# Folding row pairs in place one pass ahead, instead of inside the forward line transform

## What is computed

```python
xf = jnp.fft.rfft2(x, axes=(1, 2), norm='ortho')          # H and W; W keeps 65 modes
xf = xf.reshape(b, h, wf, NUM_BLOCKS, BLOCK)              # 8 blocks of 96 channels
o1r = relu(xr @ w1[0] - xi @ w1[1] + b1[0])               # per block, 96x96
o1i = relu(xi @ w1[0] + xr @ w1[1] + b1[1])
o2r = o1r @ w2[0] - o1i @ w2[1] + b2[0]
o2i = o1i @ w2[0] + o1r @ w2[1] + b2[1]
o2r, o2i = softshrink(o2r, 0.01), softshrink(o2i, 0.01)
out = jnp.fft.irfft2(xc, s=(H, W), axes=(1, 2), norm='ortho') + x
```

## Time and profile before

| what | value |
|---|---|
| median of three runs | 5846.9 us (5845.65 to 5852.03) |
| the profiled execution's own time | 5840.84 us |
| its span, first to last instruction | 5838.6 us |
| busy share of TensorE matmuls, VectorE, ScalarE, GpSimd | 93%, 62%, 35%, 36% |
| mean granted TensorE clock | 0.976 of full speed |

### The profile page before, as it was taken

The page is one execution under the profiler, slowest core; times in us unless marked ns, Lnnn a source line. Parts: engine busy times, 40 slices in busy tenths (PEclk is TensorE's granted clock), DMA queues, the critical chain, the costliest instruction groups (busy, mean ns, idle before and its releaser), DMA issues.

```text
span 5838.6 us, 114567 instructions
## 1 busy us (share of the span) xinstructions
PE 5407.1 (93%) x44352; PEld 4374.4 (75%) x44352; DVE 3593.4 (62%) x5379; ACT 2044.7 (35%) x3504; POOL 2079.6 (36%) x1572
## 2 busy tenths in 40 slices
PE   7999999999999999999999999999999999999998
PEld 6777777778777777777777777777777777777777
DVE  4666566665666656666566665566655666556665
ACT  2333333333333333333333333333333333333333
POOL 3442234422344323443234432344322343223432
PEclk9999999999999999999999999999999999999999
DMA  3331133311333213332133321233312333113311
GB/s 95 88 92 44 48 88 88 92 45 48 88 88 92 55 37 88 88 92 68 30 82 88 92 75 31 75 88 92 87 28 65 88 92 88 40 53 88 92 45 44
DMA packets 1065694, 421.18 MB, mean 72 GB/s; under 512 B 1062816, under 2 KB 1062944, under 8 KB 1065120
## 3 DMA queue, kind: packets, MB, share of 16 engines
q1 hardware_dynamic: 1060384, 411.62, 26.4%
q10 hardware_dynamic: 4736, 1.60, 0.1%
HBM read 210.26 MB, written 201.33 MB: 70 GB/s over the span
## 4 chain that ended last, share of the span: by engine, by line
PE 48%; issue 31%; DVE 12%; POOL 8%; ACT 1%; DMA 0%; SPq 0%; POOLq 0%; DVEq 0%; ACTq 0%
PE ps L472 8%; PE ps L393 6%; PE ps L409 6%; PE ps L436 5%; PE ps L453 4%; POOL ring_h L719 4%; PE ps L464 4%; PE ps L421 3%; DVE ring_a L285 3%; DVE x L683 3%; DVE ring_a L284 3%; PE ps L445 3%; PE ps L439 3%; PE ps L380 2%; POOL x L746 2%
## 5 line engine op out<-in xcount | busy, mean ns | idle before, releaser
L719 POOL TENSOR_TENSOR ring_h<-ydg,ones 128x512 f32<-128x512 f32 (+1 forms) x320 | 426.0, 1344 | 3056.4 <-DVE ydg L669 2653.5
L659 DVE TENSOR_TENSOR shrink_or_v<-ps,wts 128x768 f32<-128x768 f32 (+1 forms) x544 | 501.2, 921 | 1323.3 <-PE ps L472 1323.3
L537 ACT COPY ydg<-ps 127x512 f32<-127x512 f32 (+6 forms) x1056 | 581.6, 562 | 993.5 <-PE ps L381 571.1
L380 PE MATMUL ps<-tab,ring_a 128*64 128x128 f32 x6144 | 756.4, 282 | 183.5 <-DVE ring_a L285 146.7
L380 PEld LDWEIGHTS ps<-tab,ring_a 128*64 128x64 f32 x6144 | 698.1, 142 | 235.6 <-issue 172.9
L393 PE MATMUL ps<-tab,ring_h 128*128 128x128 f32 x6144 | 757.9, 290 | 115.0 <-DVE ring_h L704 115.0
L393 PEld LDWEIGHTS ps<-tab,ring_h 128*128 128x128 f32 x6144 | 751.8, 206 | 124.4 <-DVE ring_h L704 124.4
L472 PE MATMUL ps<-wts,hbig 128*128 128x192 f32 x4160 | 821.6, 340 | 0.0
L381 PE MATMUL ps<-tab,ring_a 128*63 128x128 f32 x6144 | 762.0, 283 | 0.0
L472 PEld LDWEIGHTS ps<-wts,hbig 128*128 128x128 f32 x4160 | 661.0, 189 | 122.3 <-issue 122.3
L284 POOL TENSOR_TENSOR ring_a<-x 128x256 f32<-128x256 f32 (+1 forms) x416 | 561.8, 1350 | 408.6 <-DMA x<-in_x 223.4
(11 more groups left out here) (52 smaller groups left out, 7345.5 us busy)
## 6 DMA issues: line engine op xcount, KB each, us to landing
x<-in_x SPq DMA_DIRECT2D x128, 1536.0 KB, 12.4
out<-x SPq DMA_DIRECT2D x352, 480.0 KB, 4.7
out<-x SPq DMA_DIRECT2D x32, 432.0 KB, 4.1
wts<-in_mix SPq DMA_DIRECT2D x16, 513.0 KB, 3.9
out<-x SPq DMA_DIRECT2D x32, 240.0 KB, 4.3
out<-x SPq DMA_DIRECT2D x32, 192.0 KB, 4.3
ydg<-row ACTq DMA_DIRECT2D x32, 48.0 KB
yedge<-row ACTq DMA_DIRECT2D x32, 0.8 KB
```

The source lines that it names most:

```text
L380: pe.matmul(o[0:HALF], slot[:, 0:HALF], mat("fwd_w"), start=True, stop=True)
L537: act.copy(*line_moves(stage, g)).then_inc(line_act, 1)
L719: pool.tensor_tensor(dst, src, one, ALU.mult).then_inc(packed_pool, 1)
```

## The change

The fold leaves the forward stage. During the mixing of pass q, in iterations 4 to 10, VectorE folds the image of pass q + 1 in its own buffer, in seven blocks of ten row pairs: a sum in place of the upper rows, and then a `scalar_tensor_tensor` (a product with a constant and an addition in one instruction) in place of the mirrored ones, -2 times the row plus the sum, which is the difference. Rows 0 and 64 are doubled. What fills `ring_a` is then a plain transposing copy, by ScalarE or VectorE; the first six of a pass by ScalarE in iterations 11 to 16 of the mixing before it. GpSimd packs nothing any more, neither ring. In the rows stage, where x now is folded and doubled, the sum and the difference of u and v with half of it are formed in another order: VectorE 0.5*xm + v and 0.5*xp + u (the latter into `ucopy`, four buffers), both straight from PSUM; GpSimd their sum; VectorE, two groups later, their difference. ScalarE copies no v. The mixing's last unit writes another PSUM bank and waits for `merged` in place of the bias of unit 15. The transform table changes in values only.

```diff
 def packer_a(g):
-    return "pool" if g % 3 == 0 or g < RING_A else "dve"
+    return "act" if g < RING_A + 2 or g % 3 == 2 else "dve"
 def packer_h(g):
-    if g < RING_H:
-        return ("pool", "act", "pool", "act", "pool", "pool")[g]
-    return ("dve", "act", "pool")[g % 3]
+    return "act" if g < RING_H or g % 3 == 2 else "dve"
 def mover(stage, g):
-    if stage == 0:
-        return "dve" if g % 4 == 3 else "act"
+    if stage == 0 and g < 4:
+        return "act"
     return "dve" if g % 2 else "act"
+FOLD_ROWS = 10
+FOLDS = -(-HALF // FOLD_ROWS)
+FOLD_AT = 4
+PACK_AT = FOLD_AT + FOLDS
...
+        def line_pack_moves(p, g):
             c, n = LINE_GROUPS[g]
-            engine.tensor_tensor(slot[:, :, 0:HALF], rows(1, HALF + 1), rows(H - 1, HALF - 1, -1), ALU.add)
-            return engine.tensor_tensor(slot[:, :, HALF:127], rows(1, HALF), rows(H - 1, HALF, -1), ALU.subtract)
+            return ring_a[g % RING_A][:, 0:n, 0:127], xs[p][:, 1:128, c:c + n].rearrange("p h c -> p c h")
...
+        def out_bank(u):
+            return E_BANK if u == NU - 1 else OUT_BANK
...
 # TensorE
                 def forward_lines(q, p):
-                    pe.wait_ge(y_ready, NF * q + NF - 3)
+                    pe.wait_ge(uv_ready, NF * q + NF - 3)
+                    pe.wait_ge(pairs_folded, FOLDS * (q + 1))
...
-                            pe.wait_ge(y_ready, NF * q + NF - 3 + (g + 1) // 2)
+                            pe.wait_ge(uv_ready, NF * q + NF - 3 + (g + 1) // 2)
...
                 def mix2_rows(q, u):
-                    if u:
+                    if u == NU - 1:
+                        pe.wait_ge(merged, q + 1)
+                    elif u:
                         pe.wait_ge(bias_done, NU * q + u)
...
                 def rows(q, g):
                     if g >= 4:
-                        pe.wait_ge(y_ready, NF * q + NF + g - 3)
+                        pe.wait_ge(uv_ready, NF * q + NF + g - 3)
...
 # ScalarE
+                def pack_lines(q, p, g):
+                    if g >= RING_A:
+                        act.wait_ge(line_done, lines_before(q, 0, g - RING_A) + 1)
+                    act.copy(*line_pack_moves(p, g)).then_inc(line_packed_act, 1)
...
+                            if PACK_AT <= it < PACK_AT + RING_A and not (last and p == PAIRS - 1):
+                                act.wait_ge(pairs_folded, FOLDS * (q + 2))
+                                pack_lines(q + 1, 1 - p, it - PACK_AT)
...
                         for g in range(RING_H):
-                            if packer_h(g) == "act":
-                                act.copy(*pack_moves(g, 0, LATE)).then_inc(packed_act, 1)
+                            act.copy(*pack_moves(g, 0, LATE)).then_inc(packed_act, 1)
...
-                            act.copy(vcopy[g % 3][:, 0:b - a, :].rearrange("p h c -> p (h c)"),
-                                     ps[:, 2 * (g % 4) + 1, 0:(b - a) * CB]).then_inc(v_copied, 1)
...
 # VectorE
+                def fold(q, p, i):
+                    a, b = fold_rows(i)
+                    xp, xm = xs[p][:, a:b, :], mirror(xs[p], a, b)
+                    if i == 0:
+                        edges = xs[p][:, 0:HALF + 1:HALF, :]
+                        dve.tensor_tensor(edges, edges, edges, ALU.add)
+                    dve.tensor_tensor(xp, xp, xm, ALU.add).then_inc(pair_sums, 1)
+                    dve.wait_ge(pair_sums, FOLDS * q + i + 1)
+                    dve.scalar_tensor_tensor(xm, xm, -2.0, xp, ALU.mult, ALU.add).then_inc(pairs_folded, 1)
...
+                def add_halves(q, p, g):
+                    dve.wait_ge(v_done, NF * q + g + 1)
+                    dve.scalar_tensor_tensor(xm, xm, 0.5, v[:, 0:b - a, :], ALU.mult, ALU.add)
                     dve.wait_ge(u_done, NF * q + g + 1)
+                    if g >= 4:
+                        dve.wait_ge(y_ready, NF * q + NF + g - 3)
+                    for h in (0, HALF):
+                        if HG * g <= h < HG * g + HG:
+                            dve.scalar_tensor_tensor(xs[p][:, h, :], xs[p][:, h, :], 0.5, u[:, h - HG * g, :],
+                                                     ALU.mult, ALU.add)
+                    dve.scalar_tensor_tensor(ucopy[g % 4][:, 0:b - a, :], xs[p][:, a:b, :], 0.5, u[:, lo:lo + b - a, :],
+                                             ALU.mult, ALU.add).then_inc(uv_ready, 1)
+                def subtract(q, p, g):
                     dve.wait_ge(plus_ready, NF * q + g + 1)
-                    dve.tensor_tensor(xp, u, xp, ALU.add)
-                    dve.wait_ge(minus_ready, NF * q + g + 1)
-                    dve.tensor_tensor(xm, u[:, a - HG * g:b - HG * g, :], xm, ALU.add).then_inc(y_ready, 1)
+                    dve.tensor_tensor(xm, ucopy[g % 4][:, 0:b - a, :], xm, ALU.subtract).then_inc(y_ready, 1)
...
+                            if FOLD_AT <= it < FOLD_AT + FOLDS and not (last and p == PAIRS - 1):
+                                if it == FOLD_AT:
+                                    dve.wait_ge(x_loaded[1 - p], (t + 1 + p) * 16 * LOADS)
+                                fold(q + 1, 1 - p, it - FOLD_AT)
...
+                        for g in range(NF + 2):
+                            if g < NF:
+                                add_halves(q, p, g)
+                            if g >= 2:
+                                subtract(q, p, g - 2)
...
 # GpSimd
                         for g in range(NF):
                             a, b = odd_rows(g)
-                            pool.wait_ge(v_copied, NF * q + g + 1)
-                            pool.tensor_tensor(xp, xp, vcopy[g % 3][:, 0:b - a, :], ALU.add).then_inc(plus_ready, 1)
+                            pool.wait_ge(uv_ready, NF * q + NF + g + 1)
+                            pool.tensor_tensor(xs[p][:, a:b, :], ucopy[g % 4][:, 0:b - a, :], mirror(xs[p], a, b),
+                                               ALU.add).then_inc(plus_ready, 1)
```

More of the change, by code:

```diff
@@ L193, in build @@
         clamped = [shrink_or_v[:, (2 + j) * 8 * CB:(3 + j) * 8 * CB] for j in range(2)]
-        vcopy = [shrink_or_v[:, j * HG * CB:(j + 1) * HG * CB].rearrange("p (h c) -> p h c", c=CB) for j in range(3)]
+        ucopy = [shrink_or_v[:, j * HG * CB:(j + 1) * HG * CB].rearrange("p (h c) -> p h c", c=CB) for j in range(4)]
         edge = sb("edge", [128, 2, 2 * CB])
@@ L537, in lines @@
                             act.copy(*line_moves(stage, g)).then_inc(line_act, 1)
-                        n = g + RING_H
-                        if stage == 1 and n < NG and packer_h(n) == "act":
-                            pack(q, n)
+                        n = g + (RING_H if stage else RING_A)
+                        if n < NG and (packer_h if stage else packer_a)(n) == "act":
+                            if stage:
+                                pack(q, n)
+                            else:
+                                pack_lines(q, p, n)
                 def move_row0(q):
@@ L568, in relu, with step @@
                                    bias=b1[:, 0:1]).then_inc(hid_ready, 1)
-                act.wait_ge(cleared, 2)
-                with act.Fori(0, STEPS) as t:
+                def step(t, last):
                     for p in range(PAIRS):
@@ L574, in _ @@
                         move_row0(q)
-                        lines(q, 0)
+                        lines(q, p, 0)
                         if p == 0:
@@ L658, in shrink @@
                         dve.wait_ge(shrunk, NU * q + u - 1)
+                    else:
+                        dve.wait_ge(y_ready, NF * q + NF)
                     dve.tensor_tensor(parts(v), d, b2, ALU.add).then_inc(bias_done, 1)
@@ L705, in _ @@
                         lines(q, p, 1)
-                        for g in range(NF):
-                            finish(q, p, g)
+                        for g in range(NF + 2):
[3 more added lines that the diff above has]
+                                subtract(q, p, g - 2)
+                dve.memset(yedge[:], 0.0).then_inc(cleared, 1)
+                dve.memset(clamped[0][0:1, 0:1], 0.0).then_inc(uv_ready, NF)
@@ L709, in _ @@
+                dve.memset(clamped[1][0:1, 0:1], 0.0).then_inc(y_ready, NF)
+                dve.wait_ge(uv_ready, NF)
+                dve.wait_ge(y_ready, NF)
+                dve.wait_ge(cleared, 1)
+                dve.wait_ge(x_loaded[0], 16 * LOADS)
+                for i in range(FOLDS):
+                    fold(0, 0, i)
+                with dve.Fori(0, STEPS - 1) as t:
+                    step(t, False)
+                step(STEPS - 1, True)
             @block.gpsimd
             def _(pool):
-                def fold_first(p):
-                    for g in range(RING_A):
-                        if packer_a(g) == "pool":
-                            fold(pool, p, g).then_inc(folded_pool, 1)
@@ L716, in pack, with step @@
-                def pack(g, *slots):
-                    dst, src = pack_moves(g, *slots)
```

(21 more changed lines are left out.)

91 lines of the change are left out of this document (38 added, 53 removed).

## The result

The changed kernel takes 5489.5 us (median of four runs, 5488.1 to 5495.5) against 5846.3 (5841.3 to 5852.0): the ratio is 0.939, with a 95% interval of 0.9375 to 0.9408. It is faster by 357 us or 6.1%; the forecast was 5548 us, in a range of 5480 to 5640. The profiled execution took 5488.4 us, span 5486.1.

A forecast was written before the change was run, and what follows sets the result against it. The prediction took VectorE to set the forward stage; 248 + 57 - 5 = 300 us off the profiled 5840.8 gave 5541, and with the runs' median 6 us above that execution, 5548 us, range 5480 to 5640.

The forecast's parts named there:

- The forward stage: Forward lines: with plain copies for the fold, 22.3 us against 30.3, 8.0 a pass, 248 us for 31 passes.
- The mixing: Mixing stage: stays TensorE's; VectorE's folded blocks of 2.2 us fit with slack 1.5 us, so zero cost.
- The upper price: Fold in the mixing: `scalar_tensor_tensor` at twice the addition's 1.06 us, costing about 0.6 us a pass, 19 us.
- The mixing's end: End of the mixing: with GpSimd silent, VectorE's clamps and subtraction return 1.8 us a pass, 57 us for 32.
- The inverse lines: Inverse stage: VectorE 16 us and ScalarE 13 us of work against TensorE's 21.5 or more, so nothing gained or lost.
- I keep the low clock: Before the inverse lines: TensorE's still time shrinks from 3.59 to about 3.3 us in one piece, so the low clock stays.
- the first rival: Inverse lines: the clock doesn't fall before them, as the stall is shorter; 1.8 us a pass, 5490 us; chance 0.13.
- The rows: Rows stage: VectorE leaves about when it did, TensorE at its own 1.6 us a group, so nothing gained or lost.
- The start: First pass, from the image's landing to the mixing: 43 us against 38, a loss of 5 us.
- the forecast with its small errors: Whole kernel: the forecast time within 5520 to 5565 us; chance 0.58.
- The fourth rival: Rows: `scalar_tensor_tensor` at half rate also from PSUM, 1.07 us for 480 elements, making the kernel slower, 5880 us; chance 0.06.
- The third: Forward stage: ScalarE's copies slower than 1.09 us or hand-overs adding 0.3; half the gain lost, 5670 us; chance 0.09.

The follow-up runs named there:

- b3_no_pool: The kernel before, with GpSimd folding only the six first groups and packing nothing, VectorE and ScalarE doing the rest: 5743.0 us, ratio 0.982.
- e6_pool_busy: The changed kernel with twelve never-read additions of 256 elements on GpSimd in each forward stage: 5510.0 us.
- e4_fold_plus1: The changed kernel with one more never-read addition of 512 elements on VectorE behind each of the seven folded blocks: 5495.8 us.
- e2_one_bank: The changed kernel with the mixing's last unit in the same PSUM bank as the others again, waiting for unit 15's bias: 5485.4 us.
- e1_warm: The changed kernel with twelve more never-read 128x128 matmuls on TensorE between the mixing's end and the first inverse line: 5443.7 us, ratio 0.931 to the kernel before.
- e3_late_wait: The changed kernel, with TensorE's matmuls of the rows' group g waiting for u and v of group g - 3 in place of g - 4: 5517.2 us.
- b4_warm_before: The kernel before with fifteen more never-read 128x128 matmuls on TensorE ahead of the first inverse line: 5785.8 us against 5842.2, ratio 0.991.
- e7_fold_pool: The changed kernel with the next image's fold on GpSimd in place of VectorE, computing something else at the same cost: 5539.6 us.

## Why the prediction was right, and where it was short

- **The forward stage** was the main term: 22.3 us forecast, 22.1 measured, 8.0 forecast and 8.3 gained. The order of ScalarE's moves and copies held to half a microsecond, and no slot but the first pass's was late. Half wrong was the reason I gave for the slow fold. GpSimd's contention is real in the rows, but b3_no_pool shows that without it the stage is 29.5 us, and e6_pool_busy that with some of it the new stage is 22.3. VectorE's amount of work was the bound, and taking it out of the stage is the gain. How much of the gain is the fold's leaving and how much the new division, in which ScalarE copies 8 of the 20 groups, isn't shown; no kernel has the one without the other. ScalarE's table load cost nothing behind a jump, but not because it was hidden, as I had argued: the changed kernel has none there.
- **The mixing** hides the fold, as said: 2.2 us a block, priced by the addition, 1.15 and 1.16 us a half. The upper price didn't come true. The slack of 1.5 us that I gave the small part's copy is right behind most blocks, and it is 2.1 behind the first two; VectorE is idle for 0.85 us in such a unit, and e4_fold_plus1 fills 0.6 of it with the mixing unchanged.
- **The mixing's end**: 1.8 forecast, 1.9 measured, and by GpSimd's silence (b3_no_pool). The bank saves nothing (e2_one_bank).
- **The inverse lines** were costed at nothing and gave 0.5 us. The step that fell short is "I keep the low clock", as the stall would be about 3.3 us. It is 2.85, and the clock fell in 23 of the 32 passes only, for 3.4 or 6.8 us: a pass's inverse lines take 22.2, 23.8 or 24.8. The 3.3 was a slip: TensorE stood still in two pieces, 1.1 (the row below) and 3.59 us, and 4.7 less the 1.8 gained is 2.9. Nor did the clock fall behind the stall, as I read the earlier trace rows: it fell at 2882.26, inside a stall that lasts to 2885.01. The stretches of 6.8 us in the changed kernel begin inside it too, those of 3.4 us only 0.3 to 1.5 us after the first inverse line. What this gained is a part of the first rival, 17 of its 57 us; e1_warm gives the rest.

```profile
PE ps L464 <- DVE shrink_or_v L659: 36.5, 32, 1.1
```

- **The rows** were costed at nothing and gave 0.8 us a pass, 25 us in all, the largest miss. I had read the 22.6 us of the earlier trace rows as a fixed price of the jump, and "TensorE is at its own pace" left out that the jump can be hidden. It was the wait ahead of it that was late. `uv_ready` releases it 2.2 us sooner than `y_ready` did; e3_late_wait gives 1.4 of the 1.6 us back by delaying that wait alone.
- **The start** cost 4.3 us for 5 forecast. From the first image's landing (22.95 us) to the mixing it is 43.4 us for 43 forecast, though ScalarE's table load, which the forecast had ahead of the wait, came behind it with its 1.28 us.

The two underrated terms, 42 us, and the 8 and 4 us of the others make up, to within a microsecond or two, the 53 us between the 300 forecast and the 353 measured in the span. (The sum's own terms give 5547, not 5548.) So the main terms came out by their mechanism, and the total of 5489.5 lies in the range, but below the 5520 to 5565 of the forecast with its small errors. That it equals the 5490 of the first rival is chance: that rival's condition held in 9 of 32 passes, and the rows, which no rival had, gave more than it did.

The fourth rival (slower, by a half-rate instruction from PSUM) needed 1.03 us an instruction; it is 0.65. The third (ScalarE's forward stage) needed copies clearly slower than 1.09; they are 1.10, and ScalarE is busy for 16 of the 22 us.

## What to carry to other kernels

Preparatory work on an engine that sets a stage belongs beside a stage of another engine, and the price of moving it is read from the idle time in one unit there, not from a share of the span. Here two engines that take turns at SBUF cost little as long as the slowed one had idle time: first ask for the amount of work, then for the contention. Where TensorE must wait for some 3 us, as here (2.85 and 3.59), matmuls that nobody reads can keep its clock at 2.4 GHz; they gave 46 us, to 5443.7 us, the fastest kernel of this study.

## What the runs showed of the hardware that was not expected

- Behind a jump back to the loop's start, TensorE's first matmul follows 4.1 to 5.5 us after the release of its last wait ahead of the jump (the kernel before, the changed one and e3_late_wait), and the jump shows as a gap of 0 to 2 us depending on how early that release comes. In b4_warm_before it took 5.8.
- After the same 2.85 us stall the granted clock stays at 2.4 GHz in 9 of 32 passes, and in others is 1.2 GHz for 3.4 or 6.8 us; small edits elsewhere shift how many, which moves the time by up to 13 us (e6_pool_busy).
- GpSimd's time doesn't scale with the element count alone: its addition of 960 elements takes 2.20 us with VectorE idle and 2.4 to 2.8 while they take turns (e7_fold_pool), where one of 256 into transposed order takes 1.04 alone, and one of 256 from contiguous data 0.83 on average beside VectorE's copies (e6_pool_busy).
